# Sums over d by four 32-row tiles of the array, once a chunk, in the banks of layer 1, and x0 turned with all 128 rows

## What is computed

```python
e = stack([tbl_i[ids[:, i]] for i in range(39)], axis=1)     # b, f=39, d=16
x0 = xk = e
for W in (f0, f1, f2):                                       # 128 maps each
    z = einsum('bfd,bgd->bfgd', x0, xk).reshape(b, f * g, d)
    xk = einsum('bpd,pm->bmd', z, W); outs.append(xk)
z = sum(concatenate(outs, axis=1), axis=-1)
h = relu(concatenate([z, dense_ctx], axis=1) @ W_top1 + b_top1)
y = relu(h @ W_top2 + b_top2) @ W_top3
```

## Time and profile before

| | |
|---|---|
| median of 3 runs | 687.12 us (686.92 to 687.2) |
| the profiled execution | 682.79 us, its span 680.6 us |
| busy in the span: PE, DVE, POOL, ACT | 637.7, 554.0, 513.7, 331.8 us |
| records: PE, DVE, POOL, ACT | 2704, 1689, 486, 1142 |

### The profile page before, as it was taken

One profiled execution on the slowest core, in us unless ns is written; L12 is line 12 of the kernel. 1 busy time (PEld: TensorE's weight loads), 2 busy tenths in 40 slices (PEclk: granted clock), 3 DMA queues, 4 the chain that ended last, 5 costly groups with the idle time before them and its releaser, 6 DMA issues.

```text
span 680.6 us, 10126 instructions
## 1 busy us (share of the span) xinstructions
PE 637.7 (94%) x2704; PEld 472.2 (69%) x2704; DVE 554.0 (81%) x1689; ACT 331.8 (49%) x1142; POOL 513.7 (75%) x486
## 2 busy tenths in 40 slices
PE   0199999999999999999999999999999999999998
PEld 0056777677787777777777777777777777777763
DVE  4169898989886798989886798989896798989900
ACT  3034546455553556555553555555453455556602
POOL 5759988888885789889885689888885686656610
DMA  6467414040403104040403204040402204000000
GB/s 212 99 170 233 120 11 120 7 124 2 129 3 90 40 2 128 3 128 2 120 12 71 59 2 129 4 127 3 115 17 51 77 4 125 2 0 2 0 1 0
DMA packets 57742, 43.34 MB, mean 64 GB/s; under 512 B 37355, under 2 KB 40683, under 8 KB 57558
## 3 DMA queue, kind: packets, MB, share of 16 engines
q1 hardware_dynamic: 51586, 37.99, 19.4%
q0 software_dynamic: 5120, 1.32, 2.7%
q10 hardware_dynamic: 980, 3.39, 1.4%
HBM read 40.75 MB, written 1.94 MB: 63 GB/s over the span
## 4 chain that ended last, share of the span: by engine, by line
PE 73%; DVE 13%; POOL 6%; issue 3%; ACT 3%; DMA 2%; SPq 1%; DVEq 0%; POOLq 0%; ACTq 0%
PE strip L640 15%; PE strip L644 15%; PE strip L641 15%; PE acc L604 14%; DVE scaled L446 9%; PE misc L656 5%; PE acc L667 4%; ACT first L542 2%; POOL added L350 2%; POOL found L333 2%; DVE x_diag L421 1%; PE strip L667 1%; POOL added L353 1%; PE strip L735 1%; PE misc L612 1%
## 5 line engine op out<-in xcount | busy, mean ns | idle before, releaser
L446 DVE SCALAR_TENSOR_TENSOR scaled<-strip,x_t,scaled 128x128 f32<-128x128 f32 x1216 | 330.7, 336 | 20.9 <-PE strip L644 20.8
L640 PE MATMUL strip<-w_hi,x_hi 128*128 128x512 f32 (+1 forms) x640 | 295.6, 462 | 0.7 <-issue 0.7
L644 PE MATMUL strip<-w_hi,x_lo 128*128 128x512 f32 (+1 forms) x640 | 247.8, 387 | 0.0
L641 PE MATMUL strip<-w_lo,x_hi 128*128 128x512 f32 (+1 forms) x640 | 247.7, 387 | 0.0
L542 ACT ACTIVATE product<-strip,x_t 128x128 f32<-128x128 f32 x512 | 146.9, 373 | 177.3 <-PE strip L644 175.0
L343 POOL TENSOR_TENSOR added<-added,product 128x512 f32<-128x512 f32 x128 | 170.4, 1331 | 80.5 <-ACT product L542 78.7
L333 POOL DMA_INDIRECT found<-in_tables,rows x160 | 171.4, 1071 | 28.2 <-issue 9.8
L640 PEld LDWEIGHTS strip<-w_hi,x_hi 128*128 128x128 f32 x640 | 120.4, 188 | 42.4 <-issue 11.2
L641 PEld LDWEIGHTS strip<-w_lo,x_hi 128*128 128x128 f32 x640 | 120.7, 189 | 39.7 <-issue 17.3
L644 PEld LDWEIGHTS strip<-w_hi,x_lo 128*128 128x128 f32 x640 | 120.1, 188 | 24.2 <-DVE x_lo L408 0.4
L401 DVE TENSOR_TENSOR z<-shifted,x_thrice 117x512 f32<-117x512 f32 x112 | 103.2, 922 | 22.3 <-DMA shifted<-x_fields 17.1
(11 more groups left out here) (53 smaller groups left out, 237.3 us busy)
## 6 DMA issues: line engine op xcount, KB each, us to landing
shifted<-x_fields SPq DMA_DIRECT2D x112, 234.0 KB
x_thrice<-x_fields SPq DMA_DIRECT2D x16, 234.0 KB
found<-in_tables,rows POOLq DMA_INDIRECT x160
w<-in_L_rec_f SPq DMA_DIRECT2D x1, 2496.0 KB, 11.2
g_sum<-in_L_rec_f ACTq DMA_DIRECT2D x4, 512.0 KB, 8.3
x_once<-x_fields SPq DMA_DIRECT2D x16, 78.0 KB
x_fields<-found SPq DMA_DIRECT2D x16, 72.0 KB
wt<-in_W_top SPq DMA_DIRECT2D x1, 768.0 KB, 11.4
```

The costliest lines, as they stand in the source:

```text
L446: dve.scalar_tensor_tensor(into, strip[:, q % Y_BANKS, j, :], x0_t[:, c % 2, s, f:f + 1], onto, ALU.mult, ALU.add).then_inc(scale_step, 1)
L640: pe.matmul(into, x1_hi[:, c % 2, columns], hi, start=True, stop=False)
L641: pe.matmul(into, x1_hi[:, c % 2, columns], lo, start=False, stop=False)
L644: pe.matmul(into, x1_lo[:, c % 2, columns], hi, start=False, stop=True).then_inc(strip_ready, 1)
```

## The change

The sums of a whole chunk are now made at one place, slot 9 of the next chunk, and by row tiles of the array: rows 0-31, 32-63, 64-95 and 96-127 hold two examples each, and a tile's matmul is 32 rows by 80 columns (2 examples x 40). For each of the four subs there are four such matmuls, one for each row tile, and the four tiles write into four different banks. Those banks are four consecutive turns of the ring of layer 1, which gets a seventh bank: `misc` is gone. ACT empties the four banks with four copies of 320 columns. The last chunk makes the sums of its first three subs at slot 38 and those of the fourth at the end.

`x0_diag` shrinks to 2 examples a row and sub and is made by one DVE instruction a chunk (slot 20). `x0_once` gets 128 rows, of which 39 are filled and the rest set to zero at the start; its four transposes now take all 128 rows, at slot 6, into `acc0` before layer 0 needs it. Layer 2 is five fields in each of eight slots instead of four in ten. The dense inputs are turned in `acc0` too.

```diff
-Y_BANKS = 6
+Y_BANKS = 7
...
-TURN_X0_AT = 24
-KEEP_X0_T_AT = 26
-SUMS_AT = [18, 28, 38, SLOTS + 8]
-SUMS_LATE_AT = [22, 28, 38, SLOTS + 8]
-DIAGONAL_AT = [5, 13, 22, 32]
-LAYER2_AT = range(11, 21)
-LAYER2_STEP = 4
+TURN_X0_AT = 6
+KEEP_X0_T_AT = 8
+DIAGONAL_AT = 20
+LAYER2_AT = range(13, 21)
+LAYER2_STEP = 5
...
+TILES = 4
+TILE_ROWS = P // TILES
+TILE_B = SB // TILES
+TILE_COLUMNS = TILE_B * FG
+SUMS_AT = 9
+LAST_SUMS_AT = 38
...
+def slot_of_strip(q):
+    return q + TILES * sums_before(q)
...
-                at_least(pool, g_ready, u - SUBS + 1)
+                at_least(pool, g_ready, u // SUBS)
...
-            def diagonal(c, s):
+            def diagonal(c):
...
-                    x0_diag[:, s, :, 0:FIELDS], x0_t[:, c % 2, s:s + 1, :].to_broadcast([P, SB, FIELDS]),
+                    x0_diag[:, :, :, 0:FIELDS],
...
-                act.copy(g_sum[:, :, at:at + SB], sums.rearrange("g (b f) -> g f b", b=SB)).then_inc(g_kept, 1)
+                for t in range(TILES):
+                    found_sums = strip_flat[:, (slot_of_sums(e) + t) % Y_BANKS, 0:TILE_COLUMNS * (end - begin)]
+                    act.copy(kept[:, t, :, :, :], found_sums.rearrange("g (s b f) -> g f s b", b=TILE_B, f=FG)
+                             ).then_inc(g_kept, 1)
...
-                    last = pe.transpose(x0_t_bank[:, s, :], x0_once[:, c % 2, P * s:P * s + P],
-                                        ident[0:FIELDS, 0:FIELDS])
+                    last = pe.transpose(x0_t_bank[c > 0][:, s, :], x0_once[:, c % 2, P * s:P * s + P], ident[:])
...
-            def sum_products(c, s):
-                pe.wait_ge(x2_t_ready, SUBS * c + s + 1)
-                pe.wait_ge(diag_ready, SUBS * c + s + 1)
...
-                pe.matmul(sums, x2_t[:, s, :], x0_diag[:, s, :, :].rearrange("p b f -> p (b f)"),
-                          start=True, stop=True).then_inc(g_ready, 1)
+            def sum_products(e):
...
+                pe.wait_ge(x2_t_ready, SUBS * c + end)
+                pe.wait_ge(diag_ready, c + 1)
+                for t in range(TILES):
+                    drained(slot + t - Y_BANKS)
+                for s in range(begin, end):
+                    into = slice(TILE_COLUMNS * (s - begin), TILE_COLUMNS * (s - begin + 1))
+                    for t in range(TILES):
+                        of = slice(TILE_ROWS * t, TILE_ROWS * t + TILE_ROWS)
+                        last = pe.matmul(strip_flat[:, (slot + t) % Y_BANKS, into], x2_t[of, s, :],
+                                         x0_diag[of, s, :, :].rearrange("p b f -> p (b f)"), start=True, stop=True,
+                                         tile_position=(TILE_ROWS * t, 0))
+                last.then_inc(g_ready, 1)
```

More of the change, by code:

```diff
@@ L127, in build_program @@
         x0_thrice = sb("x0_thrice", [ROWS, 2, N])
-        x0_once = sb("x0_once", [FIELDS, 2, N])
+        x0_once = sb("x0_once", [P, 2, N])
         shifted = sb("shifted", [P, T0, N])
@@ L163, in build_program @@
         acc0 = bank("acc0", [MAPS, N])
-        misc = bank("misc", [P, N])
-        sums = misc[:, 0:SB * FG]
-        x0_t_bank = misc[:, SB * FG:SB * FG + SUBS * FIELDS].rearrange("p (s f) -> p s f", s=SUBS)
         strip_flat = strip[:, :, :, :].rearrange("p y j m -> p y (j m)")
[L168 to L173, removed]
+        x0_t_bank = [of.rearrange("p (s f) -> p s f", s=SUBS)
+                     for of in (strip_flat[:, Y_BANKS - 1, :], acc0[:])]
+        dense_bank = acc0[0:D, :]
+        last_banks = [strip_flat[:, (slot_of_sums(CHUNKS) + t) % Y_BANKS, :] for t in range(TILES)]
+        h1_bank = [acc0[:]] + [strip_flat[:, (slot_of_sums(CHUNKS) - 3 + m) % Y_BANKS, :] for m in range(3)]
+        acc2 = [acc0[:, 0:P]] * (QUARTERS - 1) + [last_banks[0][:, 0:P]]
+        h2_bank = [last_banks[1], last_banks[2]]
+        y_bank = last_banks[3][0:1, :]
         ids_in = sem("ids_in")
@@ L445, in scale @@
                         dve.wait_ge(scale_step, scaled_before(u, g) + j - PER_STRIP + 1)
-                    dve.scalar_tensor_tensor(into, strip[:, q % Y_BANKS, j, :], x0_t[:, c % 2, s, f:f + 1], onto,
+                    dve.scalar_tensor_tensor(into, strip[:, slot_of_strip(q) % Y_BANKS, j, :], x0_t[:, c % 2, s, f:f + 1], onto,
                                              ALU.mult, ALU.add).then_inc(scale_step, 1)
+            dve.memset(x0_once[:], 0.0).then_inc(once_zeroed, 1)
             dve.memset(dense_t[:], 0.0).then_inc(dense_zeroed, 1)
@@ L481, in _ @@
                             sum_x1(c + 1)
-                    if n in DIAGONAL_AT:
-                        diagonal(c, DIAGONAL_AT.index(n))
+                    if n == DIAGONAL_AT:
+                        diagonal(c)
                     if g in BY_DVE[s]:
@@ L541, in scale @@
                 for j, f in enumerate(strip_fields(g)):
-                    last = act.activation(into[:, j, :], strip[:, q % Y_BANKS, j, :], ACT.Copy,
+                    last = act.activation(into[:, j, :], strip[:, slot_of_strip(q) % Y_BANKS, j, :], ACT.Copy,
                                           scale=x0_t[:, c % 2, s, f:f + 1])
@@ L569, in _ @@
                             keep_x0_t(c + 1)
[L570 to L573, removed]
+                    if c and n == SUMS_AT:
+                        keep_g(c - 1)
+                    if c == CHUNKS - 1 and n == LAST_SUMS_AT:
+                        keep_g(c)
                     if closes_quarter(c) and n == KEEP_OUT1_AT:
@@ L579, in _ @@
                         scale(c, s, g)
[L580 to L582 removed]
+            keep_g(CHUNKS)
             keep_out1(QUARTERS - 1)
@@ L624, in layer1 @@
             def layer1(c, s, g):
-                q = SLOTS * c + STRIPS * s + g
-                if q >= Y_BANKS:
-                    drained(q - Y_BANKS)
+                slot = slot_of_strip(SLOTS * c + STRIPS * s + g)
+                if slot >= Y_BANKS:
+                    drained(slot - Y_BANKS)
                 first_strip = s == 0 and g == 0
@@ L636, in layer1 @@
                     pe.wait_ge(w1_lo_ready, of_strip[-1] // W1_PIECE + 1)
-                into = strip[:, q % Y_BANKS, 0:len(of_strip), :].rearrange("p j m -> p (j m)")
+                into = strip[:, slot % Y_BANKS, 0:len(of_strip), :].rearrange("p j m -> p (j m)")
                 hi = w1_hi[:, of, :].rearrange("p f m -> p (f m)")
@@ L729, in _ @@
             pe.wait_ge(wt2_in, 16)
-            drained(last_strip - 1)
-            drained(last_strip)
             for k in range(H1 // P):
@@ L770 @@
     arrays["ident"] = np.eye(P, dtype=np.float32)
-    arrays["mask"] = np.repeat(np.eye(SB, dtype=np.float32), D, axis=0)
+    arrays["mask"] = np.tile(np.repeat(np.eye(TILE_B, dtype=np.float32), D, axis=0), (TILES, 1))
     tables = [arrays.pop(f"tbl_{f}") for f in range(FIELDS)]
```

98 lines of the change are left out of this document (60 added, 38 removed).

## The result

The kernel after takes 664.47 us (median of 4 runs, 664.38 to 665.41), the kernel before 687.02 us (4 runs, 686.78 to 687.2) beside it: a ratio of 0.968, with an interval of 0.9658 to 0.9702. That is 22.5 us less, where 7.4 less were forecast. The profiled execution took 664.53 us, its span 662.7.

What follows compares the result with a forecast made beforehand. PE's matmuls, one behind the other, were taken to bound the chunks. Sums -1.9, wait -5.0, turn -2.0, banks +1.0, end +0.5 gave -7.4 us, 687.1 to 679.7; own range 674 to 685, range of all 669 to 690.

Steps and rivals of the forecast that it cites:

- The old sums: On PE: 64 sums of 0.54 us each are removed, 34.6 us.
- The old waits: PE's sum at slot 8 waits for POOL's last `x2_t`; ten such waits go, 5.0 us less.
- The turn: PE's transposes of x0 take 0.44 us instead of 0.57, 15 times: 2.0 us less.
- The change of shape: Each of 17 blocks of sums changes the array's shape and back, 0.33 us each: 5.6 us more.
- The record: Each of 512 tile records on PE takes r = 0.053 us, the bare load; with shape changes 32.7 us, 1.9 gained.
- 512 r - 34.5: The change in us in general, r being one tile record's time on PE; nothing at r = 0.067.
- Banks: PE waits a little in slots 9 and 10 for strips' banks to be drained: 1.0 us more, ends 0 and 3.
- The end: After the last `x2_t`, one sub's sums and four short copies precede layer 2: 0.5 us more.
- B: Rival: streams and loads of different tiles run under one another, r = 0.034, 671 us; chance 0.23.
- C: Rival: the tiles go one behind the other on PE, r = 0.071, +1.9, 689.0 us; chance 0.20.
- D: Rival: each record's load stands in the open on PE, r = 0.13, +32, 719 us; chance 0.08.
- E: Rival: PE waits 1.5 us a chunk in slots 9 to 15 because DVE stays late, 695 us; chance 0.07.

Runs made afterwards that it cites:

- e5: The kernel before with the last sum of each chunk at slot 9 of the next chunk instead of slot 8: 680.12 us, ratio 0.9904.
- e6: The kernel after with the four transposes of x0 over 39 rows and 39 columns again, at the new place: 665.94 us, ratio 0.9691.
- e2: The kernel after with each sums matmul of 80 columns split into two of 40: 680.15 us, ratio 0.9901.
- e3: The kernel after with half of the 128 maps left out of the sums, 64 weight columns instead of 128: 664.69 us, ratio 0.9688.
- e8: The kernel after with the turn of x0 as two transposes of 78 filled rows instead of four of 39: 663.84 us, ratio 0.9664.
- e11: The kernel of e3 with DVE's first two products for layer 0 at slots 8 and 10 instead of 6 and 9: 652.94 us, ratio 0.9587.
- e1: The kernel after with each block's tile matmuls grouped by row tile, all four subs of one tile before the next: 700.27 us, ratio 1.0188.
- e7: The kernel after with two row tiles of 64 rows by 160 columns instead of four of 32 by 80, x0_diag twice as large: 668.75 us, ratio 0.9738.
- e4: The kernel after with sums as four matmuls of 128 rows by 320 columns and x0_diag at its old size: 685.92 us, ratio 0.9988.

## Why the prediction was off

The direction was right and the size was not: 22.5 us less for 7.4, and 664.5 us is below the range's 669. By its steps:

- **The old sums, 34.6 us out:** held (0.54 to 0.56 us at slots 18, 28 and 38).
- **The old waits, 5.0:** held; 5.4 at slot 8 in the traces, and 5.3 at slots 8 and 9 by e5.
- **The turn, 2.0:** held: 1.8 at the turn's slots in the traces, and 1.8 back by e6. The time of 0.44 us taken from the dense turn is what came.
- **The change of shape, 0.33 a block:** near. A block is 1.27 us, less 32 x 0.028: 0.37.
- **The record, r = 0.053: this step failed.** It was 0.028, or 512 x 0.025 = 12.8 us of the 15 that the forecast lacked. I wrote "streams hidden under one another, loads not" and took for the load the pace of the transposes, 0.06 us. The streams are hidden, but so are the loads, and their pace was wrong in the opposite sense. A load of these records takes 0.112 us for 128 columns, nearly twice the transposes' (by e2 the pace ignores the stream, by e3 it goes with the weights' columns); and the loads of four tiles run beside each other, which no row of before could show. 0.112 us by four tiles is 0.028. The "half of a stream" of the bound below took each tile to wait for the second record of the one ahead; in fact four records start together, one of each tile, and the next four a load later. The formula 512 r - 34.5 itself holds: with 0.028 it gives -20.2.
- **Banks, 1.0:** 1.4 at slot 10. Near, but for the wrong reason to be content: DVE was said to have the diagonals' time to give, and it is just in time (e3, e8 to e11).
- **The end, 0.5:** nothing to be seen; behind the last strip both traces have 35.9 us.
- **Not in the sum:** 2.0 us that the first step of layer 2 had waited for at slot 11 in chunks 4, 8 and 12.
- **The bounds:** by its own terms (r from 0.045 to 0.062, banks 0 to 3) the forecast's own range is 675 to 686 us, not 674 to 685. Nothing hangs on it.

Of the rivals B came: full overlap of streams and loads, with 671 us at r = 0.034; it was sized by the stream alone. What I set against it, "the load pace of 0.06", was evidence from transposes of another shape. The Trainium skill says in "TensorE: Matmul & The Clock Gate", section "LDWEIGHTS (loading the stationary operand)", that a load takes its columns at 1.2 GHz, 107 ns for 128. I called that contradicted. For these records the trace agrees with it: the step is 112 ns with 128 columns, and 69 with 64, where the load alone would be an estimated 53 by the page, the first two loads of a tile stand 55 apart, and the stream is longer. It goes on disagreeing for the transposes, 0.06 us apart. And the same page's section "The mechanism" says that tiles load and multiply in parallel, with starts about 4 ns apart; the trace agrees on the overlap, but has the starts 7 ns apart. Both rules together give an estimate of 107/4 = 27 ns a record, for the 28 measured; I had weighed them one at a time, each against the other's rival.

C and D fell by the pace in the trace; that order decides (e1) is the real form of C: grouped by tile the same records are slower than the kernel before. E fell for this kernel, but e3 and e8 show the bound that it named 0.2 us away.

## What to carry to other kernels

Interleave matmuls over the row tiles, one of each in turn: in these runs four tiles then share the time of one weight load, and the pace is the larger of a load (the kernel after) and a stream (e3, e7), divided by the tiles; grouped by tile, the gain is lost and the clock may go with it. When a wait is taken for a term, see whether it can be had by itself: one slot of delay gave the old kernel 6.6 us (e5). Before an estimate takes a pace from other instructions, ask which of load and stream set it there, and whether it can be shared. When a stretch gets shorter and the time doesn't, compare the traces slot by slot and look at the engine that drains its banks just there, whatever its share of the whole: moving two products of 0.6 us freed 5.9 us (e3 against e11).

## What the hardware showed that I had not expected

- The load of a float32 tile record with 128 columns takes 0.112 us a step, with 64 at most 0.069, where the stream sets the pace (its first two loads stand 0.055 apart); float32 transposes of 39 rows, also 128 columns, step at 0.06. Why the transposes are faster was not tried.
- Four records for four tiles begin 7 ns apart. With eight records of one tile in a row, the next tile begins beside the fifth of them, and no sooner (e1, at 514 ns).
- The granted clock fell to the 1.2 GHz level behind nine of 15 blocks of 2.7 us of tile records (e1), behind one of 15 in e2, where most are of 2.1 us and this one, with its pause, of 2.7, and behind none of 1.3 us (the kernel after). Four matmuls of all 128 rows, 2.2 us (e4), left it at 1.00 too. TensorE was busy throughout in the stretch shown, and the clock came back by itself under strips.
